# Products with the values in four runs for each group of heads, a ring of 14 score tiles, and new costs for the planner that sets the order

## What is computed

```
xn = layernorm(x)
q, k, v = split_heads(xn @ Wq.T), split_heads(xn @ Wk.T), split_heads(xn @ Wv.T)
q, k = rope(q), rope(k)
probs = softmax(where(causal, q @ k.T / sqrt(16), -1e9))
attention = merge_heads(probs @ v) @ Wo.T
xm = mix of three neighbouring tokens of xn
h = xm @ W1[p] + b1[p]                      # 9 paths of 64
paths = h @ W2[p] + b2[p]
best = argmax(tanh(xm @ Wo1 + bo1) @ Wo2 + bo2)
out = x + attention + layernorm(xn + paths[best]) * gamma + beta
```

## Time and profile before

| | |
|---|---|
| median of three runs | 817.83 us (816.98 to 821.49) |
| the profiled execution | 820.42 us |
| its span, first to last instruction | 818.1 us |
| mean granted TensorE clock | 0.962 |
| PE busy | 765.1 us, 94% |
| DVE busy | 657.5 us, 80% |
| ACT busy | 451.0 us, 55% |
| POOL busy | 289.9 us, 35% |

### The profile page before, as it was taken

The page is one execution under the profiler, slowest core; times in us unless marked ns, Lnnn a source line. Parts: engine busy times, 40 slices in busy tenths (PEclk is TensorE's granted clock), DMA queues, the critical chain, the costliest instruction groups (busy, mean ns, idle before and its releaser), DMA issues.

```text
span 818.1 us, 12610 instructions
## 1 busy us (share of the span) xinstructions
PE 765.1 (94%) x4416; PEld 363.7 (44%) x4416; DVE 657.5 (80%) x1894; ACT 451.0 (55%) x780; POOL 289.9 (35%) x459
## 2 busy tenths in 40 slices
PE   4769998999999999899999999899999999999996
PEld 2423334344455433345455443335355553354434
DVE  5988799788798788888988788888988878877722
ACT  2362543765556653775466654476556665654672
POOL 1001022891335122593244313387161502030622
PEclk9965899999999999999999999999999999999999
DMA  6368041213612524022550715022550515100013
GB/s 232 107 169 162 1 89 22 68 62 85 127 28 40 116 83 78 30 79 73 106 82 2 155 54 107 1 69 78 117 104 2 107 50 103 25 13 2 6 22 77
DMA packets 40576, 59.96 MB, mean 73 GB/s; under 512 B 4813, under 2 KB 36830, under 8 KB 37634
## 3 DMA queue, kind: packets, MB, share of 16 engines
q1 hardware_dynamic: 36002, 54.39, 28.1%
q0 software_dynamic: 4224, 4.19, 3.4%
q10 hardware_dynamic: 288, 0.59, 0.2%
HBM read 42.04 MB, written 16.85 MB: 72 GB/s over the span
## 4 chain that ended last, share of the span: by engine, by line
PE 81%; DVE 11%; ACT 3%; DMA 2%; POOL 1%; issue 1%; SPq 0%; POOLq 0%; ACTq 0%; DVEq 0%
PE bank L1548 16%; PE bank L1510 15%; PE bank L1529 15%; PE bank L1501 9%; PE bank L1491 7%; PE bank L1453 5%; PE bank L1576 3%; PE bank L1464 3%; PE bank L1471 2%; ACT prob L1123 2%; DVE bank L1341 2%; PE bank L1558 2%; DVE piecemax L1344 1%; PE bank L1519 1%; PE bank L1478 1%
## 5 line engine op out<-in xcount | busy, mean ns | idle before, releaser
L1123 ACT ACTIVATE prob<-bank 128x512 f32<-128x512 f32 x576 | 326.1, 596 | 249.8 <-PE bank L1529 245.4
L1341 DVE CUSTOM_DVE_ANT_0 bank<-bank,causal_sb 128x384 f32<-128x384 f32 (+3 forms) x512 | 241.2, 510 | 48.3 <-PE bank L1510 46.5
L1510 PE MATMUL bank<-k_st,q_st 96*128 96x512 bf16 (+3 forms) x768 | 239.3, 341 | 8.4 <-DMA q_st<-scratch 4.5
L1005 POOL TENSOR_SCALAR_AFFINE_SELECT prob<-prob 128x256 f32<-128x256 f32 (+1 forms) x320 | 132.7, 456 | 263.1 <-ACT prob L1123 260.0
L1529 PE MATMUL bank<-q_st,k_st 98*128 98x512 bf16 (+3 forms) x768 | 216.6, 335 | 7.1 <-ACT prob L1123 3.2
L1344 DVE TENSOR_REDUCE piecemax<-bank 128x1 f32<-128x512 f32 x256 | 166.0, 683 | 28.9 <-PE bank L1510 28.4
L1548 PE MATMUL bank<-prob,v_sb 128*17 128x512 f32 (+3 forms) x1536 | 159.6, 502 | 0.1
L1510 PEld LDWEIGHTS bank<-k_st,q_st 96*128 96x128 bf16 x768 | 72.1, 99 | 145.7 <-DVE piecemax L1341 36.4
L1529 PEld LDWEIGHTS bank<-q_st,k_st 98*128 98x128 bf16 x768 | 71.0, 99 | 113.9 <-ACT prob L1123 53.8
L1501 PE MATMUL bank<-w_sb,mid 128*128 128x256 f32 (+1 forms) x320 | 85.3, 388 | 0.4 <-DVE z L1332 0.3
L1453 PE MATMUL bank<-xnT,wqk_sb 128*128 128x512 f32 x128 | 68.1, 637 | 6.1 <-ACT xnT L1070 4.4
(11 more groups left out here) (82 smaller groups left out, 693.4 us busy)
## 6 DMA issues: line engine op xcount, KB each, us to landing
scratch<-parts SPq DMA_DIRECT2D x16, 768.0 KB, 3.8
q_st<-scratch SPq DMA_DIRECT2D x90, 128.0 KB, 6.9
k_st<-scratch SPq DMA_DIRECT2D x15, 384.0 KB, 4.7
z<-in_x SPq DMA_DIRECT2D x8, 512.0 KB, 4.1
mask<-chosen SPq DMA_DIRECT2D x16, 256.0 KB
z<-in_x POOLq DMA_DIRECT2D x8, 512.0 KB, 6.2
out<-z SPq DMA_DIRECT2D x8, 512.0 KB, 4.3
k_st<-scratch SPq DMA_DIRECT2D x15, 256.0 KB, 5.4
```

Source lines behind the costliest of these rows:

```text
L1005: nc.gpsimd.affine_select(out=d, in_=d, compare_op=ALU.is_ge, fill=0.0, base=0, pattern=pattern, channel_multiplier=-1).then_inc(masked, 1)
L1123: nc.scalar.activation(prob[:, place_of(G, i), :], ps[:, :], ACT.Exp, scale=float(DK) ** -0.5).then_inc(act_took, 1)
L1341: nc.vector.tensor_tensor_reduce(ps, ps, causal_sb[:, HALF - w:HALF], 1.0, NEG, ALU.add, ALU.max, to).then_inc(dve_took, 1)
L1510: nc.tensor.matmul(begin(("max", G, u))[:, 0:w], q_st[0:PARTS, G % STACKS, h, t * P:(t + 1) * P], k_st[0:PARTS, G % STACKS, h, k0:k0 + w], ...
```

## The change

It does five things.

- `RUNS = ((0, 1, 2), (3, 4), (5, 6), (7, 8, 9))`: all steps of a run get one due time, that of the last step of the run, so they come one behind the other where their needs are met.
- The ring has 14 places instead of 10. To make room in SBUF, the space kept for the descriptors of POOL's DMAs is set to 8192 bytes.
- The costs in the planner's tables are lower (for instance S 0.6 to 0.5, max without diagonal 0.69 to 0.6, stats 2.7 to 2.1), and SIGNAL goes from 0.12 to 0.2 us.
- WINDOW goes from 0.3 to 0.4 of a group, and STALL from 8 to 20.
- A DMA other than `place` is held back by LATE = 1.5 us in the choice, and a piece of DVE, ACT or POOL is not chosen if it would delay an earlier one of the same engine by more than SIGNAL.

No instruction that computes is added or removed; what changes is their order, and the waits that go with the ring.

```
-RING = 10
+RING = 14
...
+RUNS = ((0, 1, 2), (3, 4), (5, 6), (7, 8, 9))
...
-        for step in range(NSTEPS):
-            at = G + (last_unit(step) + LAG + 0.5) / NS
-            add(at, "pv", G, step)
-            if step in (2, NSTEPS - 1):
-                half = step_half(step)
+        for run in RUNS:
+            at = G + (last_unit(run[-1]) + LAG + 0.5) / NS
+            for step in run:
+                add(at, "pv", G, step)
+            if run[-1] in (2, NSTEPS - 1):
+                half = step_half(run[-1])
...
-SIGNAL = 0.12
+SIGNAL = 0.2
...
-        return 0.17 + MAX_UNITS[name[2]][4] * 0.00106 if has_diagonal(name[2]) else 0.69
+        return 0.11 + MAX_UNITS[name[2]][4] * 0.00101 if has_diagonal(name[2]) else 0.6
...
-WINDOW = 0.3
+WINDOW = 0.4
...
+LATE = 1.5
...
-STALL = 8
+STALL = 20
...
-                others.append((met, e, n))
-        now = max(free["pe"], best[1]) if best else 1e9
-        go = None
+                others.append((met + (LATE if e == "dma" and name[0] != "place" else 0), e, n))
+        now = max(free["pe"], best[1]) if best else free["pe"]
+        go, soon = None, {}
         for met, e, n in others:
             late = pending[0][0] >= pending[n][0] - 0.02
+            start = max(met, free[e])
+            if e in soon and start + OWN_US[pending[n][1][0]] > soon[e] + SIGNAL:
+                continue
...
-    nc = _bacc.Bacc("TRN2", target_bir_lowering=False, num_devices=1)
+    nc = _bacc.Bacc("TRN2", target_bir_lowering=False, num_devices=1, dynamic_dma_scratch_size=8192)
```

19 lines of the change are left out of this document (10 added, 9 removed).

## The result

The changed kernel takes **782.74 us** in the median of four runs (782.04 to 784.09), the kernel before 817.92 us beside it. The ratio is 0.9555, with a 95% interval of 0.9512 to 0.9598: faster by 35 us. The forecast was 798 us, with a range from 786 to 811, so the direction was right and the gain nearly twice what was foretold. The profiled execution took 784.09 us, with a span of 782.4 us and a mean granted clock of 0.974 (before 0.962).

A forecast was written before the change was run, and what follows sets the result against it. PE was taken as the bound, busy 765.1 of 818.1 us and covered throughout the long stretches. Terms -19.4 + 2 - 5 + 2.5 = -19.9 us took the median 817.8 to 798 us, range 786 to 811.

The forecast's parts named there:

- The price of a visit: On PE, a visit to the narrow matmuls costs about 0.22 us beyond its columns, paid per visit, not per step.
- term 1: In PE's row, 182 narrow stretches become 94: 88 x 0.22 = -19.4 us, with nothing hiding them.
- Term 2: Where DVE paces (second halves of groups 0, 4, 8), PE arrives earlier at banks not emptied: +2 us given back.
- Term 3: PE's waits at the layer norms, 11.6 us in all, shrink by somewhat under half: -5 us.
- Term 4: New waits behind long visits, where no bank of max or S is filled: +2.5 us, bounds nothing and 27 us.
- The clock: Rival: the granted clock falls at visits of three steps; five falls counted as +8 us, 806 us; chance 0.03.
- DVE became no bound: Rival that DVE becomes the bound, as long visits idle it and cuts may fall upon rotary products: 811 us; chance 0.12.
- TensorEngine Tiling (Array Packing), PSUM Bottleneck: Skill's rule for the DVE rival: tiling speeds TensorE but not the emptying of PSUM, which may then bound.
- The slower rival: DVE's three banks are already empty when a visit begins: 843 us at worst, 823 with half; chance 0.05.
- The case without effect: Each step pays its own way in and out, so only merging with `shift` remains: 817 us; chance 0.03.
- PE's busy falls by 17 to 19 us: Sign on PE: its busy time falls by some 17 to 19 us at the same number of matmuls.
- DVE's idle before max grows: Sign on DVE: its idle time before the lines of max grows; no size given.

The follow-up runs named there:

- split: Changed kernel's order with the units of max ahead of a run put between its steps, 124 narrow visits instead of 94: 791.02 us.
- warm: Changed kernel with some 55 more matmuls in the opening, whose result nobody reads, in gaps of PE: 781.52 us, and 783.44 us when run again.
- old_opening: Changed kernel with the opening, until group 1 is due, planned with the costs, choice and single steps of before: 788.66 us.
- take_old: Changed kernel with the old times to take a bank (0.6 instead of 0.5 us for S, 0.69 instead of 0.6 for max): 813.41 us.
- own_old: Changed kernel with the old costs of the engines' own pieces (OWN_US: stats, norm, rest, sel and so on): 812.21 us.
- planner_only: Changed kernel with single steps, the ring of 10 and the usual descriptor space, so the new planner alone: 787.66 us.
- merge: New planner's single-step order with the ring of 14, steps of pv moved back to the next of their run, 87 visits instead of 137: 802.91 us.
- banks: Changed kernel with one PSUM bank taken from max and given to S (three for S, two for max), planned anew: 822.68 us.

## Why the prediction was right and wrong

**The price of a visit and term 1 (-19.4 forecast, -25.7 measured).** That a visit costs and a step in a row doesn't was right; split shows it at 0.24 us. The count, 182 to 94, was right as well. The size was short: 25.7 / 88 = 0.29 us. The 0.22 had 0.09 for the way in and 0.12 for the way out, and left out the first f32 matmul behind it, seen to be late by 0.1 us but not added. Visits with an f32 matmul behind them fell from 33 to 13, the others from 149 to 81; at 0.33 and 0.24 us that makes 22.9 us. So 3.5 us of the miss are the price itself; the other 2.8 are time at 1.2 GHz and short waits inside visits, which the visits' part also holds (warm). This is the first of the failed steps, worth 6.3 us.

**Term 2 (+2 forecast).** The opening's waits rose by 0.3 us, so the term was 1.7 us too high. It counted visits in an unchanged order; old_opening, with 5.6 us more of waits, points to a new order that waits less there.

**Term 3 (-5 of at most 11.6 forecast).** Both long waits at the layer norms are gone (20.00 of 20.00 us covered, twice), and so is the one of 2.0 us at 139 us of the earlier trace rows. By starts of matmuls the waits there fell by 8.8 us and the clock's cost by 2.0, so -10.8. The place was right, and "somewhat under half" was the wrong choice between the ends. Its ground, that DVE's work must move out of the stretch, held: 93% busy became 85%. In part the work also shrank, which the term ("the work of DVE is the same") had left out: the time by which DVE instructions are stretched, mostly beside POOL's products, fell from 25.5 to 11.2 us in all, and instructions of the cuts that last over 0.5 us went from 13 (12.4 us above their usual length) to 6 (5.7 us). The rule of the Trainium skill (SBUF — State Buffer, Who interferes with whom), that of a VectorE instruction with two SBUF inputs and one of GpSimd that reads SBUF the later waits for the whole of the other, agrees with these rows for the cuts with two inputs. Stretching is not the whole cause: take_old has 28.2 us of it and own_old 20.1, at nearly the same time.

**Term 4 (+2.5 of at most 27 forecast).** Here the forecast was too low, and the waits that it missed are partly hidden by term 3. In the steady stretches waits rose by 8.8 us, from 19.5 to 28.3. Against planner_only, which has single steps, it is 13.8 us in all. What failed is the choice near the lower end, on the ground that DVE had 91.7 us to spare: merge, where PE waits 10.5 us for DVE instead of 4.2, points to it that they were spare on the mean and not where the visits need them. The bound of 27 us was a good one: merge pays 28.0. (The count of 87 stretches of `pv`, 19 of them with three steps, was off: in the list there are 80, 23 with three steps and 34 with two. That would have made the term hardly different.)

**The clock (a rival, 0.03, as a loss).** It went the other way, -8.5 us. 1.2 GHz held for 61.4 us of the span before and 41.0 after; in the opening it came in five pieces between 47.7 and 143.3 us before, and in one, 46.0 to 80.1, after. The prediction had the row for the opening, 0.67 on the mean, and no term for it: it put it at nothing without a reason, which is a failed step too. How much of it is a gain of its own stays open, since warm raises the clock with no certain gain.

**The sum.** -25.7 of visits, +0.3 in the opening, -10.8 at the layer norms, +8.8 in the steady stretches and -6.5 of clock outside the layer norms give -33.9; the remaining 1.8 us are waits in the tail. Against the sum of -19.9 the miss in the span is 15.8 us: 6.3 from the visits, 1.7 from term 2, 5.8 from term 3, 6.5 from the clock and 1.8 from the tail, less 6.3 for term 4. The lower end of the range, 786, let terms 2, 3 and 4 vary, but gave the visits' price and the clock no room, and these two are 12.8 us.

**The cause behind the terms.** The greater error is not in a term. The prediction treated the runs as the change and the new costs as what moves a few waits. The runs explain nothing without the planner (822.27 us), and with the new planner planner_only to the changed kernel is worth 4.9 us in the median, 7 by the ratios (8.6 in the spans: 16.2 us of visits and 6.3 of clock, less 13.8 of waits). The planner alone is worth 30. Term by term that was hidden, because fewer visits stand in the changed order whoever brought them; the planner alone brings 45 of the 88.

**The rivals.** DVE became no bound: its idle time before the maxima fell from 77.2 to 52.9 us. The rule of the Trainium skill (TensorEngine Tiling (Array Packing), PSUM Bottleneck) did not decide here, but banks shows that it is near: with one bank less for the maxima, and the order planned for that, the time is 40 us longer. The slower rival (banks dry at each visit) did not come, as units of max and a piece for DVE stand ahead of and beside a long run; merge shows it in part, without that. The case without effect (each step pays its own way) fell with split, and with the 2.16 us of a run of three. "PE's busy falls by 17 to 19 us" was 25.2; "DVE's idle before max grows" was wrong.

**What stays open.** Which single wait decides in a half with a layer norm differs from order to order, and no run isolates one. How far the cost tables, the choice and the runs add up can't be said either: they don't, since each alone changes the whole list.

## What to carry to other kernels

Where a planner with costs makes the order, try as its costs the distance from one start to the next in a full row, undisturbed, and not the mean duration that a profile shows for one instruction; compare a "x2" row with the mean of one, and the mean with the middle value. Price a saved switch between modes by undoing it in place, and then count the waits that the longer run brings, on the engines that starve during it as well: merging in a finished order lost 28 us of waits for 16.7 us of switches, and the planner that knew of the runs lost 13.8 for 16.2. And when a diff changes both a structure and the numbers of a planner, cost them apart, however small the numbers look.
